# Dummy matmuls on zeros ahead of the first stage, and a new order for the edge means and the weight scales

## What is computed

```python
def hypergraph_conv(x, adj, W, b):
    H = (adj != 0)                       # [N, C, C], nodes x hyperedges
    w = adj[:, 0, :]                     # the first row weighs the hyperedges
    Dn = 1 / einsum('nce,ne->nc', H, w)  # 0 where the sum is 0
    Be = 1 / H.sum(axis=1)
    m = Be * einsum('nce,nch->neh', H, x @ W.T)      # edge means
    return Dn * einsum('nce,neh->nch', H, m) + b

h = relu(layernorm(x))
u = layernorm(relu(hypergraph_conv(h, adj, W1, b1)), gamma, beta)
out = x + (hypergraph_conv(u, adj, W2, b2) + h)
```

## Time and profile before

| | |
|---|---|
| median of 3 runs | 639.96 us |
| the runs | 637.48, 640.06, 639.96 us |
| the profiled execution | 639.25 us |
| its span, first to last instruction | 637.4 us |
| mean granted TensorE clock | 0.997 |
| busy: TensorE, VectorE, ScalarE, GpSimd | 620.3, 473.3, 290.9, 111.6 us |

### The profile page before, as it was taken

One profiled execution on the slowest core, in us unless ns is written; L12 is line 12 of the kernel. 1 busy time (PEld: TensorE's weight loads), 2 busy tenths in 40 slices (PEclk: granted clock), 3 DMA queues, 4 the chain that ended last, 5 costly groups with the idle time before them and its releaser, 6 DMA issues.

```text
span 637.4 us, 11994 instructions
## 1 busy us (share of the span) xinstructions
PE 620.3 (97%) x4808; PEld 467.7 (73%) x4808; DVE 473.3 (74%) x1148; ACT 290.9 (46%) x540; POOL 111.6 (18%) x132
## 2 busy tenths in 40 slices
PE   2999899999999999999999999999999999999998
PEld 2756758688586885778766886768858688586887
DVE  6999878976599665995779948798478876388632
ACT  4476743463435535364353632646334363125620
POOL 0115029230310304004040040401212012000000
PEclk9999989999999999999999999999999999999999
DMA  8995870069800697109940099203990159000701
GB/s 336 260 348 105 143 320 4 31 144 179 339 34 1 160 201 301 34 1 204 258 201 34 26 222 299 116 34 84 205 364 10 34 111 213 9 1 2 197 3 67
DMA packets 146215, 89.78 MB, mean 141 GB/s; under 512 B 134896, under 2 KB 135536, under 8 KB 141168
## 3 DMA queue, kind: packets, MB, share of 16 engines
q1 hardware_dynamic: 146160, 89.02, 51.8%
HBM read 47.06 MB, written 8.39 MB: 87 GB/s over the span
## 4 chain that ended last, share of the span: by engine, by line
PE 90%; DVE 6%; ACT 2%; DMA 1%; issue 0%
PE acc L583 18%; PE acc L600 18%; PE acc L523 15%; PE acc L564 12%; PE acc L544 11%; PE acc L503 7%; PE acc L505 7%; PE acc L485 2%; DVE z L940 1%; DMA z<-z_split_ring 1%; DVE incidence L876 1%; DVE stat L945 1%; DMA x_in<-x 1%; ACT z L673 1%; ACT z_split_ring L672 1%; ACT residual L649 1%
## 5 line engine op out<-in xcount | busy, mean ns | idle before, releaser
L583 PE MATMUL acc<-xw_split,incidence 128*128 128x256 f16 x1024 | 113.2, 273 | 0.0
L600 PE MATMUL acc<-edge_means,incidence_t 128*128 128x256 f16 x1024 | 113.1, 273 | 0.0
L583 PEld LDWEIGHTS acc<-xw_split,incidence 128*128 128x128 bf16 x1024 | 100.1, 98 | 13.2 <-DVE xw_split L976 0.2
L600 PEld LDWEIGHTS acc<-edge_means,incidence_t 128*128 128x128 bf16 x1024 | 100.2, 98 | 13.1
L630 ACT ACTIVATE edge_means<-acc,edge_inverse 128x256 f16<-128x256 f32 x128 | 55.4, 474 | 116.8 <-PE acc L583 69.9
L503 PE MATMUL acc<-h_split,incidence 128*128 128x257 f16 x448 | 98.6, 273 | 0.0
L505 PE MATMUL acc<-h_split,incidence 128*128 128x256 f16 x448 | 98.6, 273 | 0.0
L523 PE MATMUL acc<-incidence_t,edge_means 128*128 128x512 bf16 x448 | 97.8, 379 | 0.0
L564 PE MATMUL acc<-w_split,z 128*128 128x256 f16 x768 | 87.2, 276 | 2.2 <-DMA z<-z_split_ring 2.2
L564 PEld LDWEIGHTS acc<-w_split,z 128*128 128x128 f16 x768 | 75.8, 99 | 12.3 <-issue 2.5
L544 PE MATMUL acc<-w_split,pt_split 128*128 128x512 f16 x384 | 84.2, 379 | 0.0
(11 more groups left out here) (104 smaller groups left out, 636.9 us busy)
## 6 DMA issues: line engine op xcount, KB each, us to landing
adj_in<-adj SPq DMA_DIRECT2D x32, 1024.0 KB, 10.4
out<-residual SPq DMA_DIRECT2D x32, 256.0 KB, 2.6
x_in<-x SPq DMA_DIRECT2D x7, 1024.0 KB, 5.5
edge_weights<-adj SPq DMA_DIRECT2D x7, 512.0 KB, 3.7
x_in<-x SPq DMA_DIRECT2D x2, 512.0 KB, 4.5
z<-w1t SPq DMA_DIRECT2D x1, 512.0 KB, 12.5
xw_split<-w2t SPq DMA_DIRECT2D x1, 512.0 KB, 13.3
incidence_t<-incidence SPq DMA_TRANSPOSE x32, 4.9
```

The lines of the kernel that those rows point to most:

```text
L583: last = nc.tensor.matmul(acc[:, 0:DOUT], inc[:, b.slot, ct, P * et:P * (et + 1)], xw[:, ct, part, :], start=(ct == 0 and part == HI), sto ...
L600: last = nc.tensor.matmul(acc[:, 0:DOUT], inc_t[:, b.slot, ct, et, :], edge[:, et, part, :], start=(et == 0 and part == HI), stop=(et == T ...
```

## The change

TensorE gets 22 matmuls (`BUSY`) of 512 columns ahead of the first A stage. Their operands are the first tile of `edge`, which GpSimd sets to zero, and their result goes to the last PSUM bank, which stage A overwrites. They begin when the first half of x has landed.

On VectorE the first edge means go ahead of the maximum of W2 and of `split_weights`, and the W1 factor goes behind the layer norm statistics of the next batch. On ScalarE the two scaled copies of W1 go behind `root_x` and the first two `drain_b`.

```diff
--- before.py
+++ after.py
@@ -94,6 +94,7 @@
     BIAS_BANK, DEGREE_BANK = 7, 6
     WPARTS = 3
     CT_FIRST = 6
+    BUSY = 22
     PER_BATCH = 5 * T + 4
 
     with ExitStack() as ctx:
@@ -197,6 +198,7 @@
         rows_loaded = sem("rows_loaded")
         stored = [sem(f"stored{q}") for q in range(QUARTERS)]
         ones_set = sem("ones_set")
+        zeros_set = sem("zeros_set")
         max_here = sem("max_here")
         max_all = sem("max_all")
         bias_step = sem("bias_step")
@@ -384,6 +386,7 @@
         @block.gpsimd
         def _(pool):
             nc.gpsimd.memset(h0[:, :, ONE:ONE + 1], 1.0).then_inc(ones_set, 1)
+            nc.gpsimd.memset(edge[:, 0, :, :], 0.0).then_inc(zeros_set, 1)
 
             def add_h0(b):
                 for t in range(T):
@@ -428,6 +431,14 @@
 
         @block.tensor
         def _(pe):
+            def keep_busy():
+
+                pe.wait_ge(zeros_set, 1)
+                pe.wait_ge(x_first, 16)
+                for _ in range(BUSY):
+                    nc.tensor.matmul(acc_ring[:, RING - 1, :], edge[:, 0, HI, 0:P],
+                                     edge[:, 0, :, :], start=True, stop=True)
+
             def first_stage_a():
 
 
@@ -603,6 +614,7 @@
                     last.then_inc(f_done, 1)
 
 
+            keep_busy()
             first_stage_a()
             first_stage_b()
             stage_c(Batch(0, 0))
@@ -763,12 +775,12 @@
             last.then_inc(gamma_w2, 1)
             for et in range(T):
                 t1_hi_part(b0, et)
+            root_x(b1_)
+            drain_b(b0, 0)
+            drain_b(b0, 1)
             act.wait_ge(w1_scale, 5)
             copy(w1s[:, :, HI, :], w1f, scale=wr[:, 2:3])
             copy(w1f, w1f, scale=wr[:, 2:3]).then_inc(w_hi, 1)
-            root_x(b1_)
-            drain_b(b0, 0)
-            drain_b(b0, 1)
             for g in range(GROUPS):
                 h0_tiles(b1_, g)
                 h0_hi_part(b1_, g)
@@ -1091,18 +1103,18 @@
             for g in range(GROUPS):
                 ts = slice(GT * g, GT * (g + 1))
                 V.tensor_tensor(res[:, 0, ts, :], x_in[:, ts, :], res[:, 0, ts, :], ALU.add).then_inc(x_added, GT)
-            split_weights()
             dve.wait_ge(w1_loaded, 16)
             largest(0, w1f)
-            dve.wait_ge(gamma_w2, 1)
-            largest(1, gf).then_inc(max_here, 1)
             for half in range(2):
                 edge_inverse(b0, half)
                 for et in range(T // 2 * half, T // 2 * (half + 1)):
                     t1_lo_part(b0, et)
-            factor(0, w1_scale, 1.0 / (H0_SCALE * PT_SCALE * W_SCALE))
+            dve.wait_ge(gamma_w2, 1)
+            largest(1, gf).then_inc(max_here, 1)
+            split_weights()
             x_stats(nxt)
             inverse_root(x_ln, x_step, nxt, X_STEPS, 1.0)
+            factor(0, w1_scale, 1.0 / (H0_SCALE * PT_SCALE * W_SCALE))
             b_lo(b0, 0)
             b_lo(b0, 1)
             dve.wait_ge(bias_done, 1)
```

## The result

Beside one another in twelve executions each, the changed kernel took 640.56 us (median; 639.20 to 642.00) and the kernel before 638.09 (637.27 to 640.39): an estimated ratio of 1.0033 (the quotient of the medians is 1.0039), with a 95% interval from 1.0019 to 1.0046. The profiled execution took 641.41 us.

What follows compares the result with a forecast made beforehand. TensorE was 90% of the chain, but the start-up was bound by VectorE and ScalarE. Dummies 0, VectorE's wait 0.5 and ScalarE's copies 0.9 gave +1.4 us, hence 641.0 (640.65 to 641.4); own range 640 to 642, with rivals 637.8 to 643.0.

Steps and rivals of the forecast that it cites:

- the class, the same: Whole kernel: time within about 0.5%, 3.2 us, of before, between 636.8 and 643.2; chance 88%.
- Dummies ahead of A: TensorE's start: dummies end at 11.1 to 11.3, cost nothing; stage A's last matmul starts 1.51 us earlier, at 25.49.
- VectorE: VectorE's new order to b_lo: one new 0.53 us wait for A banks, so b_lo at 36.92 instead of 36.39.
- ScalarE, the term that decides: ScalarE's queue: W1 copies from 37.04 delay the x tiles; copy of half 1 at 45.8, 1.4 us later.
- the 46.4: VectorE's L912 behind the copy of half 1: waits until 46.4, where it started at 45.05 before.
- 2.14 on GpSimd: GpSimd's low part of W1: 2.14 us after the copies, done at 41.3, ahead of stage C at 43.1.
- 1.4 us to the restart: Chain from the copy of half 1: 1.4 us go through to z's last transposed quarter and TensorE's restart, 79.47 becoming 80.9.
- After that TensorE is the chain, and nothing else has changed.: After TensorE's restart near 80.9: no further change in time to the kernel's end.
- The clock's loss: TensorE's restart in the first D stage: clock falls, 1.8 us lost; change bounded between 0 and -1.8.
- The rival that it goes away: Clock loss at 79 us disappears: 641.0 - 1.8 = 639.2; chance 22%.
- Rivals of the rise: Dummies' clock: no rise on zeros, 644.8 or 645.2, 6%; or rise late, at 6.7 us, +1.3, 642.3, 12%.
- the bound of 1.3: Stage A's start: if the clock rises at 6.7 us, dummies end at 12.9 and A is 1.3 us late.

Runs made afterwards that it cites:

- e5: Changed kernel with GpSimd's low half of W1 computed on only 16 of 1024 columns: 639.98 us, ratio 1.0013.
- e6: Changed kernel with ScalarE's two W1 copies on only 16 of 1024 columns: 639.65 us, ratio 1.0020.
- e7: Kernel before plus dummies, split of the first weights on GpSimd, b1 row's load ahead of the next batch's adjacency loads: 637.29 us, ratio 0.9978.
- e10: Kernel before plus dummies and the b1 row's load ahead of the adjacency loads: 637.79 us, ratio 0.9993.
- e12: e7 unchanged, run again on another chip beside the kernel before: 637.38 us, ratio 0.9993.
- e3: Kernel before plus dummies, VectorE doing both maxima first, then edge means, then the split of the first weights: 638.33 us, ratio 1.0006.
- e1: Kernel before plus the dummies and their memset alone: 638.44 us, ratio 1.0006.
- e2: Changed kernel without dummies and memset, the new order alone: 640.88 us, ratio 1.0041.
- e8: Kernel before plus nine dummy matmuls ahead of the wait for z's last quarter in the first D stage: 640.26 us, ratio 1.0020.
- e9: Kernel before with only the b1 row's load moved ahead of the next batch's adjacency loads: 637.62 us, ratio 0.9989.
- e11: e7 without the dummies: 637.66 us, ratio 1.0000.

## Why the prediction came out as it did

The time (641.0 for 640.56) came out, and so did the class, the same (the difference lies under the 3.2 us that the prediction named). Of the way there one half was right, and that the time fits so closely is luck. The sum was set on three executions of the kernel before with a median of 639.96; two of them lie near 640, in the group with the fall. Twelve executions gave 638.09. The change in time was forecast at 1.0 to 1.4 us and measured at 2.5 by the medians, 1.6 to 1.7 like with like.

- **Dummies ahead of A.** They end at 11.5, A runs on the fast clock, its last matmul starts at 25.68 (25.49 forecast; all is 0.17 later because x landed later). A started at 11.76 and not 11.6 by x's landing, not by the dummies. Right here, and in part by luck: the working allows a rise up to 4.0 us after the start, and in five of the nine profiles with these dummies it came 4.6 to 5.8 us after. That they "cost nothing on the path" was wrong, for a reason not in the working: in all ten profiles with added matmuls the instruction load comes earlier (below).
- **VectorE.** Edge counts at 24.23 after 0.47 us of idling (24.05 and 0.53 forecast), b_lo at 37.15 (36.92). Right.
- **ScalarE, the term that decides.** W1 copies from 37.27, copy of half 1 at 45.95 with no wait of its own (37.04 and 45.8). Right, and e5 shows the 46.4 when nothing else is in the way. The word "decides" was too strong: GpSimd's low part moved with the copies from 36.63 to 39.55, into VectorE's incidence pair, and held the same line to 46.86. The prediction had that op, as "2.14 on GpSimd", and asked only whether C gets its result in time, not whom it meets. e6 shows that this branch keeps the loss when ScalarE's is shortened.
- **1.4 us to the restart.** The delay, 1.8 us by then, went through to the last transposed quarter (issued at 75.80 and not 74.03), but not "to TensorE's restart". Before, the instruction load met that last quarter (5.30 us). After, it met the second one, for which TensorE waits until 75.11 (6.1 us). The last then landed in 3.6 us, at 79.4, while TensorE was still busy with the 72 matmuls from 75.11. So B was 0.88 late, not 1.4.
- **"After that TensorE is the chain, and nothing else has changed."** This is the step that failed: 1.3 us of the profiled pair's 2.18 come 520 us later, in the last D stage. That the load falls into the transposes there exactly in the kernels with added matmuls is shown by fourteen profiles, and that it delays a transpose by the quarters of the batches between. Why added matmuls move it so far is open. The two errors, 0.5 too much and 1.3 too little, cancel in part: 1.4 was forecast for the profiled pair.
- **The clock's loss.** It stayed within the bounds given: still there in half of the executions, 3 us earlier. Its size was 1.67 us and not 1.8: 24 matmuls at full clock take 2.78 (the row at 69.36), not 2.6. The stretches of the changed kernel, against the earlier trace rows:

```profile
76.00:77.00 1.00, 1.00 (x9) 0.78 (x7) 1.00 (x4) 0.49 (x2) 0.00 (x0) 0.73 0.30 65
77.00:78.00 1.00, 1.00 (x6) 0.75 (x5) 1.00 (x3) 0.29 (x1) 0.00 (x0) 0.50 1.21 276
...
79.00:80.00 1.00, 1.00 (x7) 0.74 (x6) 0.90 (x4) 0.42 (x1) 0.00 (x0) 0.57 0.85 164
```

  The rival that it goes away was right for the other half of the executions, though nine of twelve were without it before the change too. And e7, e10 and e12 show it nearly gone where the pause is short: the profiled executions fell after pauses of 2.22, 2.72, 2.92 and 2.97 us, and not after 2.46 or any of 1.97 and less.
- **Rivals of the rise.** The clock does rise on zeros. It does so late in other executions: in the profiles of e3, e6, e7 and e10 A started at 12.17 to 12.58 instead of e1's 11.54, inside the bound of 1.3.

What stays open: by what rule the instruction load moves (nine added matmuls moved it as 22 did), why the fall came more often with the change, and whether e12's earlier start would show in the time if the load were kept out of the last D stage. That wasn't tried.

## What to carry to other kernels

Speeding up an engine that isn't the last to arrive gains nothing until everything that ends at the same point is earlier too: here VectorE's order, ScalarE's queue, GpSimd's one instruction and one small row behind 4 MB of loads all stood within 2 us of one another. For each instruction that a reordering moves, ask not only who waits for it but whom it now runs beside. And compare the whole trace, the last batch too: adding instructions at the start can move a load of instructions into a transfer that matters at the end.

## What was not expected of the hardware

- *GpSimd can stall VectorE until its own instruction ends.* A 2.13 us subtraction on GpSimd stretched VectorE's pair from 1.28 to 2.94 us, and in e6 an operation on one column from 0.15 to 1.74, ending 0.02 us behind GpSimd. The Trainium skill (SBUF — State Buffer, "SBUF: two separate sides") says that the two engines share one pair of ports under an exclusive lock: a VectorE operation takes it in a mode that uses both ports, or with two inputs in SBUF against a GpSimd operation that reads SBUF, and the one that comes second blocks. The runs agree as far as they go: the one-column operation has two inputs in SBUF, and L912's pair, which reads a PSUM bank (`acc`), kept its 1.28 us beside the earlier trace rows. In which mode the incidence pair ran, no run shows.
- *A load of instructions costs a transposing DMA about 1 to 2 us.* In the last D stage all quarters of z land in 3.6 to 4.0 us where no 16 KB load falls among them; where one does, the slowest takes 4.8 to 5.7. In the first D stage one does in every profile, and the slowest takes 5.0 to 6.1. With dummies ahead of A it meets the second quarter; without them it meets the third (e2, e8, e9, e11) or the last (before).
- *The rise of the clock varies from execution to execution,* on zeros as on data. Stretches of the changed kernel, in which the matmuls of a microsecond go from three to six at 8 us, 2.9 us after their start, and of e7, where they go from four to seven at 11, 5.8 after it; the other runs lie between.

```profile
7.00:8.00 1.00, 1.00 (x3) 0.30 (x2) 0.95 (x5) 0.20 (x1) 0.00 (x0) 1.00 1.01 418
8.00:9.00 1.00, 1.00 (x6) 0.48 (x5) 0.83 (x7) 0.00 (x0) 0.00 (x0) 1.00 0.97 401
```

```profile
10.00:11.00 1.00, 1.00 (x4) 0.39 (x3) 1.00 (x3) 0.97 (x3) 0.00 (x0) 1.00 0.95 401
11.00:12.00 1.00, 1.00 (x7) 0.46 (x5) 0.96 (x6) 0.97 (x3) 0.00 (x0) 1.00 0.99 418
```

  The granted clock shows 1.00 in all four of these stretches: before the first rise it doesn't tell, and the spacing does.
